# ScalarE takes over the last subtraction of the first half of the inner rows in a feed-forward stage

## What is computed

```python
def _act_quant(x):
    scale = 127.0 / jnp.clip(jnp.max(jnp.abs(x), axis=-1, keepdims=True), 1e-05)
    return jnp.clip(jnp.round(x * scale), -128.0, 127.0) / scale
def _bitlinear(x, w):
    return jnp.einsum('bsi,oi->bso', _act_quant(x), _weight_quant(w))
gate = jax.nn.silu(_bitlinear(x, w_gate))          # 512 -> 2048
up = _bitlinear(x, w_up)                           # 512 -> 2048
out = _layernorm(x + _bitlinear(gate * up, w_down))    # 2048 -> 512
```

## Time and profile before

| what | value |
|---|---|
| three runs without profiling, median | 1807.12 us (1805.96 to 1807.32) |
| the profiled execution, its own time | 1808.88 us |
| its span (first to last instruction) | 1806.4 us |
| busy over the span: PE / DVE / ACT / POOL | 97% / 78% / 65% / 62% |
| mean granted TensorE clock, share of full speed | 0.992 |

### The profile page before, as it was taken

How to read it: one execution, slowest core, us unless ns; L and a number is a source line. 1 busy time by engine, 2 the same in 40 slices (tenths; PEclk the granted TensorE clock), 3 DMA queues, 4 the chain that set the end, 5 groups by cost and what they waited for, 6 DMA issues and landing times.

```text
span 1806.4 us, 37455 instructions
## 1 busy us (share of the span) xinstructions
PE 1752.7 (97%) x13942; PEld 1475.7 (82%) x13957; DVE 1412.5 (78%) x3240; ACT 1172.5 (65%) x2680; POOL 1113.4 (62%) x1250
## 2 busy tenths in 40 slices
PE   8999999999998899999999999999999999988997
PEld 7777777778877899999999999899899999974443
DVE  6777778787887677777777788777776777787888
ACT  6878887756755566666666667666666656654664
POOL 3434445664566586786686655677777788551554
PEclk9999999999998999999999999999999999999999
DMA  5223323111105423432432523314313341543553
GB/s 206 76 67 94 103 75 111 46 32 46 48 22 173 137 90 98 152 100 77 153 103 74 167 97 86 112 49 125 96 61 101 96 114 52 125 106 92 129 129 97
DMA packets 141106, 176.80 MB, mean 98 GB/s; under 512 B 63884, under 2 KB 99088, under 8 KB 140928
## 3 DMA queue, kind: packets, MB, share of 16 engines
q1 hardware_dynamic: 122392, 138.15, 25.3%
q0 software_dynamic: 14656, 28.92, 5.9%
q10 hardware_dynamic: 3880, 7.35, 1.3%
HBM read 109.25 MB, written 50.46 MB: 88 GB/s over the span
## 4 chain that ended last, share of the span: by engine, by line
PE 74%; DVE 10%; ACT 5%; POOL 5%; DMA 3%; issue 3%; ACTq 0%; POOLq 0%; DVEq 0%
PE att_ps_T L552 7%; PE att_ps_SA L1755 5%; PE att_ps_P L1731 5%; PE att_ps_SB L612 4%; PE att_ps_P L1719 4%; PE att_ps_P L552 4%; PE att_ps_P L1783 4%; PE att_ps_SB L600 3%; PE att_ps_O L1719 3%; PE att_ps_T L1719 3%; PE att_ps_P L1769 3%; PE att_ps_T L1731 3%; PE att_ps_O L1731 2%; PE att_ps_P L1794 2%; POOL sa_p_lo L423 2%
## 5 line engine op out<-in xcount | busy, mean ns | idle before, releaser
L1537 POOL TENSOR_TENSOR ca_pr<-ca_pr,ca_rec 112x750 f32<-112x750 f32 x256 | 366.6, 1453 | 187.2 <-DVE ca_rec L2017 184.3
L423 POOL TENSOR_TENSOR sa_p_lo<-sa_pr,sa_p_hi 112x448 fp32r<-112x448 f32 x128 | 146.8, 1162 | 210.5 <-ACT sa_p_hi L718 209.7
L1902 ACT ACTIVATE ca_big<-att_ps_P 126x384 fp32r<-126x384 f32 (+1 forms) x254 | 105.3, 449 | 66.1 <-PE att_ps_P L1769 64.9
L1896 ACT ACTIVATE ca_pr<-att_ps_SA,ca_nmax 112x750 f32<-112x750 f32 x128 | 113.7, 888 | 22.0 <-DVE ca_nmax L2013 11.2
L887 DVE RECIPROCAL sa_sums<-sa_sums 128x224 f32<-128x224 f32 x64 | 99.1, 1548 | 33.8 <-ACT sa_sums L727 33.6
L2022 DVE TENSOR_TENSOR ca_big<-att_ps_P,ca_big 126x384 fp32r<-126x384 f32 (+1 forms) x254 | 119.8, 498 | 6.2 <-ACT ca_big L1902 5.9
L2013 DVE TENSOR_REDUCE ca_nmax<-att_ps_SA 112x1 f32<-112x752 f32 x128 | 119.1, 931 | 1.3 <-PE att_ps_SA L1755 1.2
L2013 DVE TENSOR_REDUCE ca_nmax<-att_ps_SB 112x1 f32<-112x752 f32 x128 | 119.1, 930 | 0.0
L1731 PE MATMUL att_ps_P<-ca_w_hi,ca_ct 128*126 128x256 f32 x558 | 114.2, 284 | 1.4 <-DVE ca_q_lo L1996 1.4
L1896 ACT ACTIVATE ca_pr<-att_ps_SB,ca_nmax 112x750 f32<-112x750 f32 x128 | 113.3, 885 | 0.1
L1769 PEld LDWEIGHTS att_ps_P<-att_ident,ca_pr 64*126 64x126 f32 (+1 forms) x1524 | 85.5, 138 | 15.2 <-issue 10.8
(11 more groups left out here) (354 smaller groups left out, 6618.9 us busy)
## 6 DMA issues: line engine op xcount, KB each, us to landing
ct_kept<-ca_ct SPq DMA_DIRECT2D x8, 1134.0 KB, 9.3
ca_ct<-ct_kept POOLq DMA_DIRECT2D x8, 1134.0 KB, 7.7
ct_kept<-ca_ct SPq DMA_DIRECT2D x8, 1116.0 KB, 12.3
ca_ct<-ct_kept POOLq DMA_DIRECT2D x8, 1116.0 KB, 10.0
sa_xin<-in_x_dram SPq DMA_DIRECT2D x16, 448.0 KB, 3.7
xt_kept<-ca_xt SPq DMA_DIRECT2D x8, 896.0 KB, 5.2
ca_xt<-xt_kept POOLq DMA_DIRECT2D x8, 896.0 KB, 5.3
ternary<-ca_stage SPq DMA_DIRECT2D x36, 172.0 KB, 1.9
```

The lines of the kernel that those rows point to most:

```text
L423: pool.tensor_tensor(p_lo[:, h % NB, :], pr[:, h % NB, :], f32(p_hi[:, h % NB, :]), ALU.subtract).then_inc(p_split, 1)
L1537: pool.tensor_tensor(w, w, rec[:, h % PB, c:c + 1].to_broadcast([R, S]), ALU.mult).then_inc(norm_done, 1)
L1896: act.activation(pr[:, h % PB, c, :].rearrange("r (a s) -> r a s", a=2), two_halves(psum[slot]), ACT.Exp, bias=nmax[:, h % PB, c:c + 1], a ...
```

## The change

ScalarE's function `quantise_second(t)`, for the second half alone, becomes `quantise_hidden(t, half)` for either half. ScalarE's loop calls it for half 0 between the scaling of the two halves, from the pass with t = 3 on (tiles 2 to 12); tiles 0 and 1 stay as they were. VectorE's loop no longer quantises half 0, and does both halves of the last tile behind the loop.

```diff
-    BY_VECTOR = 3
+    BY_SCALAR = 2
...
-        def quantise_second(t):
-            act.wait_ge(h_scaled, 2 * t + 2)
+        def quantise_hidden(t, half):
+            act.wait_ge(h_scaled, 2 * t + half + 1)
             if t:
-                act.wait_ge(hqt_in[1], 16 * t)
-            act.activation(hq[:, half_of(1)], h[:, half_of(1)], ACT.Copy, bias=-ROUND).then_inc(hq_done[1], 1)
+                act.wait_ge(hqt_in[half], 16 * t)
+            act.activation(hq[:, half_of(half)], h[:, half_of(half)], ACT.Copy, bias=-ROUND).then_inc(hq_done[half], 1)
...
                 scale_hidden(t - 1, 0)
+                if t > BY_SCALAR:
+                    quantise_hidden(t - 1, 0)
                 scale_hidden(t - 1, 1)
-                quantise_second(t - 1)
+                quantise_hidden(t - 1, 1)
...
                 guess_root(t - 2, sums)
-                quantise_hidden(t, 0)
+            quantise_hidden(T - 1, 0)
             quantise_hidden(T - 1, 1)
```

## The result

The changed kernel takes 1812.35 us (median of 14 runs, 1809.6 to 1815.47) against 1808.66 us of the kernel before in as many runs beside it (1805.96 to 1811.8). The ratio is 1.0021, with a 95% interval of 1.0013 to 1.003: it is slower by 2.4 to 5.4 us. Four launches among all runs of this study took 2,398 to 9,545 us, two of them of the kernel before; they are left out of every ratio.

A forecast was written before the change was run, and what follows sets the result against it. VectorE's own queue up to hidden of f = 0 was taken to hold the kernel before, ScalarE's queue the changed one. +0.16, +2.40, +0.78 and +1.07 make +4.41 on 1807.12: 1811.5 us, range 1809.8 to 1813.2.

The forecast's parts named there:

- The place, not the work: ScalarE's queue, times after pass head S: moved subtraction between scalings delays silu f = 0 by 1.08 us; period 11.24.
- The path before: Kernel before: VectorE held by its own queue up to hidden of f = 0, at S+4.88 in a 10.91 us period.
- Tiles 3 to 11: Eight feed forward periods of 11.24 us, 89.92 against 87.52: +2.40 us.
- The last two passes: Tiles 11 to 12 and 12 to 13, without round_x: heads 11.04 us apart against 10.26 and 9.97, +0.78 and +1.07.
- Tile 2 to 3: Pass from tile 2 to 3: hidden f = 2 at 1678.39 instead of 1678.23, before held by TensorE: +0.16 us.
- VectorE's gain is 0.38 and not 1.11: VectorE's residual starts at S+1.92 instead of S+2.30, since GpSimd must first free y: 0.38 us gained.
- Rival 1: VectorE stays the bound, faster: period 10.53 us, -3.0 us over eight periods, 1804.1 in all; chance 5%.
- Rivals 2 and 3: ScalarE handovers cheaper than read, +3.2 us, 13%; or dearer, 0.27 us more in each of 11 periods, +7.4, 8%.
- The page's rule: Additions and multiplications belong on VectorE; by it the moved work is dearer by 0.37 us each, 4 in 11; not summed.
- Rival 2: Handovers on ScalarE cheaper, moved subtraction 1.06 us behind S instead of 1.17: sum +3.2, 1810.3 us; chance 13%.
- What I had counted as nothing: Turning of halves, TensorE's idle rising from 0.4 to about 0.8 us per period, clock and GpSimd: no cost.
- TensorE's own time in a period: TensorE waits 0.37 us for hidden of f = 1, so about 10.5 of 10.91 us are its own, the gain's floor.

The follow-up runs named there:

- e1: Changed kernel with both scalings first on ScalarE and both subtractions behind them: 109.22 us for tiles 3 to 13, ratio 1.0005 to the kernel before.
- e3: Changed kernel with ScalarE's subtraction of half 0 cut to 32 of 1024 columns, output wrong: period 10.53 us, ratio 0.999 to the kernel before.
- e4: Changed kernel with half 0's subtraction kept on VectorE for tiles 11 and 12: 109.53 us for tiles 3 to 13, ratio 1.001 to the kernel before.
- e8_again: The changed kernel run again unchanged: 111.70 us for tiles 3 to 13, ratio 1.0021 to the kernel before.
- e5_spread: Changed kernel reordered on ScalarE: both scalings first, one subtraction behind the first silu, x work behind later silus: ratio 0.9989 to the kernel before.
- e6_two_y: Changed kernel with scalings first, one subtraction behind the first silu, x work later, and two buffers for y: ratio 0.9985 to the kernel before.
- e9_before_two_y: The kernel before with two buffers for y and nothing moved to ScalarE: 106.86 us for tiles 3 to 13, ratio 0.9996.

## Why the prediction was right

The forecast was 1811.5 us, +4.41, in a range of 1809.8 to 1813.2. Measured were 1812.35 and +3.7 (2.4 to 5.4). Its base was the median of three runs, 1807.12; over 14 runs before has 1808.66, so part of the agreement of the absolute number is luck (with that median the forecast would have been 1813.1), and the difference is what counts. By its steps:

- *The place, not the work.* The forecast put silu f = 0 at S+4.27, measured S+4.27; `hidden` f = 0 at 5.03, measured 5.03; silu f = 2 at 6.06, measured 6.02; `hidden` f = 2 at 6.84, measured 6.79; period 11.24, measured 11.20. The 0.04 lies in silu f = 1 to `round_x`, forecast 0.59 and measured 0.57, and from there to silu f = 2, 0.63 and 0.61. e1 to e3 showed the mechanism: with the order or the length changed, the period follows.
- *The path before.* The prediction named VectorE's queue up to `hidden` of f = 0 as what holds the kernel before. The chain view takes the branch over `round_x` instead, which stood at S+4.96 behind the scale of x. The two branches lay 0.02 us apart: the buffer for silu f = 2 came free at S+5.71 (4.88 + 0.83) and the silu started at 5.73. Both hang on the residual, so the forecast does not change with it.
- *Tiles 3 to 11*: +2.40 forecast, +2.05 measured; the 0.35 between them is 8 times that 0.04. The sum of the kernel before holds one period of 11.20, by a late store, among seven of 10.90, so the steady price is 0.30 in each period, 2.4 in eight.
- *The last two passes*: +0.78 and +1.07 forecast, +0.79 and +1.09 measured; e4 gave 2.15 back by undoing these two alone, somewhat more than the 1.85 of the forecast, since both of its passes took 9.97. Against a usual 9.97 in both, the price is 1.1 in each; the 10.26, and with it the +0.78, was a chance of that one profile.
- *Tile 2 to 3*: +0.16 forecast, +0.45 in the first profile. The extra is not of the change: in e8_again, the same kernel, this pass took 11.20 instead of 11.53, +0.12. TensorE had waited 5 us for tile 1's `hidden` and its clock was low behind that wait, for a time that differs from one execution to the next (last section).
- *VectorE's gain is 0.38 and not 1.11*: the residual started at S+1.90 (1.92 forecast), behind GpSimd, with 1.27 us of wait in every steady pass. That gain went nowhere, since `hidden` of f = 0 waits 0.49 for silu.
- *Rival 1* had the right price for a case that did not come: its period of 10.53 is that of e3_thin, and e5_spread's 10.52. Rivals 2 and 3, cheaper or dearer handovers, did not happen; each handover was within 0.02 us of the one read.
- *The page's rule*, that such work belongs on VectorE (the Trainium skill, page ScalarE: Activation LUTs, section Rules for kernel authors): by the instruction alone it holds here, 0.70 against 1.06. In this loop it does not decide, since VectorE's 1.20 holds a collision with GpSimd, and e5_spread and e6_two_y, with the work on ScalarE, are both faster than the kernel before.
- *The chances*: 75% for slower by over 0.2% and 22% for less. The ratio of 1.0021 lies at the border, and its interval holds both. Rival 2 said that the period must be 0.10 to 0.13 shorter to stay under +3.6; the 0.81 between 4.41 and 3.6, over the 11 passes, is 0.07 in each, or 0.10 over eight, so the border was nearer than it said.

What I had counted as nothing held: no wait for the turned halves in the changed kernel's steady passes, clock 1.00, TensorE's wait for `hidden` 0.67 (0.8 forecast).

One reading was off without touching the sum: TensorE's own time in a period is 10.37 (e6_two_y) and not "about 10.5". The bracket of 0.37 is less than the wait cost. Groups that wait for nothing start 0.86 or 0.87 us apart; the one that waited started 1.40 behind the group ahead of it (1720.28, 1721.68), 0.54 late, and 10.91 - 0.54 is 10.37.

## What to carry to other kernels

An engine that is busy for two thirds of a loop can still be its bound: count what stands in its queue between the event that releases it and the result that others wait for, not its share. What can wait on such an engine should stand behind those results. Here the moved 1.06 us cost 2.3 us more over eight periods between the two scalings than behind them. With one subtraction behind the first silu, x behind the silus and a second buffer for `y`, the same work let the loop gain 4.0 us over ten passes. Before counting a gain on the engine that gives work away, look for the next semaphore that it will meet.

## What the runs showed of the hardware that I had not expected

- The first long product behind a wait of TensorE varies. The 16 matmuls of a down product take 3.62 us in nearly every steady pass of every profile (3.66 at most). Those of tile 1, behind a wait of 5 us, took 4.10 to 5.57 in eleven profiles, although TensorE has the same instructions in all of them, and the pass from tile 2 to tile 3 took 10.97 to 12.33. Those of the last tile, behind further waits, took 3.62 to 5.31. That spread of 1.4 us is over a third of what the change costs a launch, so a difference of two spans would mislead; the sums from tile 3 on leave it out. The row of the changed kernel, then its windows in this stretch (clock in the third field from the end), then the longest one, of e9_before_two_y:

```profile
1666.94 4.78 PE L2443 MATMUL att_ps_SA<-ff_held,ff_hqt 128*128 128x512 bf16 x16
```

```profile
1660.00:1662.00 2.00, 0.22 (x2) 0.00 (x0) 0.76 (x2) 1.39 (x3) 0.00 (x0) 1.00 0.95 285
...
1664.00:1666.00 2.00, 0.74 (x2) 0.28 (x3) 1.79 (x3) 1.96 (x4) 0.00 (x0) 0.50 0.98 249
...
1668.00:1670.00 2.00, 2.00 (x8) 0.75 (x6) 1.87 (x8) 0.09 (x1) 0.00 (x0) 0.68 0.29 66
1670.00:1672.00 2.00, 2.00 (x11) 0.89 (x10) 0.60 (x4) 1.97 (x2) 1.21 (x2) 1.00 0.00 0
```

```profile
1668.08 5.57 PE L2443 MATMUL att_ps_SA<-ff_held,ff_hqt 128*128 128x512 bf16 x16
```

In the changed kernel TensorE stands still from 1660.2 to 1665.3, the clock goes to 0.50, the level of 1.2 GHz, and comes back during the product. In windows of 1 us the clock reads 0.50 for about six of them in e9_before_two_y (1666 to 1672, product 5.57) and for three in e8_again (1671 to 1674, product 4.10).

- A store of 256 KB that lands late reaches VectorE through two semaphores. In the kernel before it also made the one long period of 11.20: GpSimd's subtraction came late (1738.23, 1.03 long) and VectorE's collided with the whole of it, 1.49 us instead of 1.20:

```profile
1738.32 1.49 DVE L2593 TENSOR_SCALAR ff_hq<-ff_h 128x1024 bf16<-128x1024 f32 x1 [0.55 <-ACT ff_h L2493]
```

- Which of the two subtractions began first decided who paid. Where GpSimd began first, it took its 1.03 and VectorE ended 0.55 or 0.56 behind GpSimd's end, whether that made 1.20 or 1.49. Where VectorE began first, it took its 0.69 and GpSimd took 1.37, and 1.58 in e9_before_two_y, where VectorE began only 0.01 us ahead.
